# A transformer layer with a mixture of experts: gate, up and router products in plain fp32, expert weights held in SBUF

## The reference, cut to what matters

```
x  = x + ln(attention(ln(x)) @ Wout) * g_out
lg = (x @ wt.T + cond @ wg.T) / 2               # router, 8 logits a token
gp = leaky(einsum('th,ehm->etm', x, w_gate))    # 8 experts, h = 256, m = 128
up = einsum('th,ehm->etm', x, w_up)
y  = sum over the two best experts of weight * ((gp * up) @ w_down)
y += (leaky(x @ sw_gate) * (x @ sw_up)) @ sw_down    # shared, 256 wide = 2 blocks
x  = x + y
```

## Time and profile before

| | us |
|---|---|
| median of 3 runs | 1060.0 (1059.67 to 1060.96) |
| the profiled execution, its own time | 1064.17 |
| its span, first to last instruction | 1062.4 |
| mean granted TensorE clock | 0.994 of full |

### The profile page before, as it was taken

How to read it: one execution, slowest core, us unless ns; L and a number is a source line. 1 busy time by engine, 2 the same in 40 slices (tenths; PEclk the granted TensorE clock), 3 DMA queues, 4 the chain that set the end, 5 groups by cost and what they waited for, 6 DMA issues and landing times.

```text
span 1062.4 us, 21427 instructions
## 1 busy us (share of the span) xinstructions
PE 1014.6 (96%) x6788; PEld 815.3 (77%) x6788; DVE 707.4 (67%) x2457; ACT 526.5 (50%) x1564; POOL 437.0 (41%) x422
## 2 busy tenths in 40 slices
PE   3887999999999999999999999999999999999998
PEld 2665877778777887778777787777877788777877
DVE  8789577665867558665676647676576755856543
ACT  3488346651565435663456614665246643565220
POOL 1634154441554333642535515454245534444212
PEclk9899999999999999999999999999999999999999
DMA  5316414112132013311132212311123211232043
GB/s 198 80 54 215 151 60 122 53 66 63 61 110 90 28 55 101 100 61 61 43 118 72 71 42 79 112 65 46 62 66 113 82 41 41 84 106 71 20 138 102
DMA packets 40996, 87.68 MB, mean 83 GB/s; under 512 B 4192, under 2 KB 19040, under 8 KB 40624
## 3 DMA queue, kind: packets, MB, share of 16 engines
q1 hardware_dynamic: 39920, 83.57, 24.5%
q10 hardware_dynamic: 960, 2.62, 0.7%
HBM read 76.57 MB, written 9.60 MB: 81 GB/s over the span
## 4 chain that ended last, share of the span: by engine, by line
PE 75%; DVE 10%; issue 5%; ACT 4%; DVEq 0%; POOL 0%; ACTq 0%
PE psY L1641 13%; PE psS L1511 6%; PE psO L1547 5%; PE psG L69 5%; PE psG L71 5%; PE psG L70 5%; PE psT L1522 5%; PE psS L71 3%; PE psS L70 3%; PE psS L69 3%; PE psS L1507 3%; PE psT L1529 2%; PE psO L1550 2%; PE psT L69 2%; PE psT L71 2%
## 5 line engine op out<-in xcount | busy, mean ns | idle before, releaser
L604 POOL TENSOR_TENSOR work<-work,rden 128x514 f32<-128x514 f32 x128 | 134.0, 1047 | 322.3 <-DVE rden L1137 321.6
L1641 PE MATMUL psY<-Wd,H 128*128 128x256 f32 x640 | 172.5, 399 | 0.0
L763 ACT ACTIVATE work<-work,low 128x257 f32<-128x257 f32 x256 | 128.5, 504 | 60.1 <-DVE low L1155 59.5
L69 PE MATMUL psG<-x1T_hi,Wgu 128*128 128x512 f32 (+1 forms) x292 | 134.8, 462 | 2.6 <-ACT leaky L807 1.9
L1641 PEld LDWEIGHTS psY<-Wd,H 128*128 128x128 f32 x640 | 112.4, 190 | 29.4 <-issue 14.4
L1155 DVE CUSTOM_DVE_ANT_0 work<-psS,bias,null_s 128x256 f32<-128x256 f32 x256 | 113.3, 480 | 28.4 <-PE psS L1511 25.9
L1251 DVE SCALAR_TENSOR_TENSOR leaky<-leaky 128x512 f32<-128x512 f32 x80 | 56.4, 704 | 101.5 <-ACT leaky L807 100.5
L71 PE MATMUL psG<-x1T_lo,Wgu 128*128 128x512 f32 (+1 forms) x292 | 114.9, 394 | 0.0
L70 PE MATMUL psG<-x1T_hi,Wgu 128*128 128x512 f32 (+1 forms) x292 | 114.4, 392 | 0.0
L593 POOL TENSOR_TENSOR rq<-qss,neghalf 128x16 f32<-128x16 f32 x32 | 97.5, 3048 | 36.3 <-DVE qss L1131 36.3
L1511 PE MATMUL psS<-KB,qT 64*128 64x256 f32 (+1 forms) x1024 | 105.7, 325 | 0.0
(11 more groups left out here) (259 smaller groups left out, 2306.7 us busy)
## 6 DMA issues: line engine op xcount, KB each, us to landing
Wgu<-wexp SPq DMA_DIRECT2D x80, 512.0 KB, 3.4
Wb<-wscr SPq DMA_DIRECT2D x64, 256.0 KB, 3.6
wexp<-Wgu SPq DMA_DIRECT2D x10, 512.0 KB, 2.9
xres<-in_x SPq DMA_DIRECT2D x8, 512.0 KB, 4.7
xin<-in_x SPq DMA_DIRECT2D x7, 512.0 KB, 4.2
out<-work SPq DMA_DIRECT2D x7, 512.0 KB, 2.9
H<-in_wgu SPq DMA_DIRECT2D x10, 256.0 KB, 3.9
bias<-bscr SPq DMA_DIRECT2D x4, 512.0 KB, 6.6
```

The costliest lines, as they stand in the source:

```text
L69: te.matmul(dst, a_hi, b_hi, start=start, stop=False)
L604: pool.tensor_tensor(T1[sl][:, hs, :], T1[sl][:, hs, :], rden[sl][:, 1, hs].unsqueeze(2) .to_broadcast([P, 2, N + 1]), ALU.mult)
L763: act.activation(T1[sl][:, h, :], T1[sl][:, h, :], ACT.Exp, scale=-1.0, bias=low[sl][:, 1, h:h + 1], accum_out=den[sl][:, 1, h:h + 1])
L1641: mm = te.matmul(psY[:, t // 2, (t % 2) * D:(t % 2 + 1) * D], H[:, k % H_RING, t * P:(t + 1) * P], Wd[:, ORDER[k], :], start=(k == 0 and t ...
```

## The change: what it does

The parts, `wexp`, the ring, the splits in round 0 and the rounds' weight loads go. The ten blocks of raw fp32 weights are loaded once into `Wgu` (ten DMAs of 256 KB, right behind the load of round 1's x), and PE waits for all ten once, between round 0 and the loop. x1 turned is one fp32 tensor: ACT copies its first chunk out of PSUM, DVE its second. A gate or up product is four plain fp32 matmuls, two halves of 256 tokens by two chunks; a half in the last round is two. The router product is two plain fp32 matmuls of 512 columns with 8 stationary columns, and its turn uses the identity. The DVE preparations of the router's parts and of I2 go.

```diff
-        x1T = [sb(f"x1T_{part}", [P, KC, TOK], F32R) for part in PARTS]
-        Wgu = sb("Wgu", [P, W_RING, 2, 2, KC, P], F32R)
+        x1T = sb("x1T", [P, KC, TOK])
+        Wgu = sb("Wgu", [P, BLOCKS, 2, KC, P])
...
-            def load_weights(m, k):
-                former = k - W_RING if k >= W_RING else max(range(k, BLOCKS, W_RING)) - BLOCKS
-                need(sp, u_ps, m, former + 1)
-                stand(sp, waited_sp)
-                sp.dma_start(Wgu[:, k % W_RING].bitcast(F32), wexp.ap()[ORDER[k]]).then_inc(wgu_ld[k % W_RING].sem, 16)
...
-            for e in range(BLOCKS + 2):
-                if e < BLOCKS:
-                    if e >= H_RING:
-                        sp.wait_ge(parts_done.sem, e - H_RING + 1)
-                    sp.dma_start(H[:, e % H_RING, :], wgu[e].rearrange("p w c m -> p (w c m)")) \
-                        .then_inc(wraw_in[e % H_RING].sem, 16)
...
+            for k in range(BLOCKS):
+                sp.dma_start(Wgu[:, k], wgu[ORDER[k]]).then_inc(ld_gu.sem, 16)
...
-                        act.activation(Wgu[:, e % W_RING, 0], H[:, e % H_RING, :].rearrange(
-                            "p (w c m) -> p w c m", w=2, c=KC), ACT.Copy).then_inc(lead_done.sem, 1)
...
-                for c, bank in ((0, psG), (1, psO)):
-                    need(act, x1T_ps, m, c + 1)
-                    act.activation(x1T[0][:, c, :], bank[:], ACT.Copy).then_inc(x1T_a.sem, 1)
+                need(act, x1T_ps, m, 1)
+                act.activation(x1T[:, 0, :], psG[:], ACT.Copy).then_inc(x1T_a.sem, 1)
...
-                        dve.tensor_tensor(Wgu[:, e % W_RING, 1], H[:, e % H_RING, :].rearrange(
-                            "p (w c m) -> p w c m", w=2, c=KC), Wgu[:, e % W_RING, 0].bitcast(F32),
-                            ALU.subtract).then_inc(parts_done.sem, 1)
...
-            def x1_parts(m):
-                for c, bank in ((0, psG), (1, psO)):
-                    need(dve, x1T_a, m, c + 1)
-                    dve.tensor_tensor(x1T[1][:, c, :], bank[:], x1T[0][:, c, :].bitcast(F32),
-                                      ALU.subtract).then_inc(x1T_v.sem, 1)
+            def x1_turned(m):
+                need(dve, x1T_ps, m, 2)
+                dve.tensor_copy(x1T[:, 1, :], psO[:]).then_inc(x1T_v.sem, 1)
...
             def logits(m, last=False):
                 for c in range(KC):
-                    te.matmul(logit_bank(last), WtP[:, c, :], x1T[0][:, c, :], start=(c == 0), stop=False, skip_group_check=True)
-                for c in range(KC):
-                    mm = te.matmul(logit_bank(last)[0:E, :], WtP[:, c, 0:E], x1T[1][:, c, :], start=False, stop=(c == KC - 1),
-                                   skip_group_check=True)
+                    mm = te.matmul(logit_bank(last), Wt[:, c, :], x1T[:, c, :], start=(c == 0), stop=(c == KC - 1))
...
             def gate_up(m, k, w, bank):
-                for c in range(KC):
-                    mm = products(te, bank, [Wgu[:, k % W_RING, part, w, c, :] for part in range(2)],
-                                  [part[:, c, :] for part in x1T], c == 0, c == KC - 1)
+                for half in range(2):
+                    cols = half_tokens(half)
+                    for c in range(KC):
+                        mm = te.matmul(bank[:, cols], Wgu[:, k, w, c, :], x1T[:, c, cols], start=(c == 0), stop=(c == KC - 1))
                 return mm
...
             attention(0, None, 1)
+            te.wait_ge(ld_gu.sem, 16 * BLOCKS)
             with te.Fori(1, ROUNDS - 1) as r:
```

More of the change, by code:

```diff
@@ L287, in logit_bank @@
         def logit_bank(last):
-            return psY[0:2 * E, 1, :] if last else psO[0:2 * E, :]
+            return psY[0:E, 1, :] if last else psO[0:E, :]
         def weight_bank(last):
@@ L330, in attention_moe @@
         bias_in = [events(f"bias_in{i}", 0) for i in range(BIAS_PARTS)]
[L331 to L334, removed]
+        ld_gu = events("ld_gu", 0)
         xin_in = events("xin_in", 16)
@@ L906, in kv_parts @@
             def kv_parts():
[L907 to L910, removed]
+                hi, lo = (part[:, :, KV0:Q0] for part in Wall)
+                pre(dve.tensor_copy(hi, Wkvn_in))
+                pre(dve.tensor_tensor(lo, Wkvn_in, hi.bitcast(F32), ALU.subtract))
                 n = wall_trail(slice(0, KC), Q0, 2 * P)
@@ L1000, in attention @@
                 if moe is not None:
[L1001 removed]
+                    x1_turned(moe)
                 else:
[L1003 removed]
                     positions_norm(8, 4, V_SILU1)
@@ L1565, in turn_half @@
                 if half > 0:
-                    need(te, x1T_v, m, KC * half)
+                    need(te, x1T_a, m, half)
+                    need(te, x1T_v, m, half)
                 for c in range(KC):
@@ L1572, in block_half @@
             def block_half(m, k, w, half):
-                need(te, wgu_ld[k % W_RING], m, 16 * (k // W_RING + 1))
-                need(te, x1T_v, m, KC * (half + 1))
+                need(te, x1T_a, m, half + 1)
+                need(te, x1T_v, m, half + 1)
                 cols = half_tokens(half)
@@ L1597, in turn_logits @@
                 for t in range(TILES):
-                    mm = te.matmul(psY[:, 0, t * E:(t + 1) * E], LT[:, t * P:(t + 1) * P], I2, start=(t == 0), stop=True,
+                    mm = te.matmul(psY[:, 0, t * E:(t + 1) * E], LT[:, t * P:(t + 1) * P], ident[0:E, 0:E], start=(t == 0), stop=True,
                                    skip_group_check=True)
```

63 lines of the change are left out of this document (14 added, 49 removed).

## The result

The changed kernel takes 1108.99 us (median of 4 runs, 1108.63 to 1110.24) against 1060.01 us of the kernel before, run beside it: a ratio of 1.0452, 95% interval 1.0440 to 1.0465 (the two medians themselves give 1.0462). The forecast was 1106, with a range of 1096 to 1118. The profiled execution of the changed kernel took 1108.63 us, its span is 1106.8.

What follows compares the result with a forecast made beforehand. PE, 96% busy and 75% of the chain, was taken to bound the kernel. Loop +44.4, tail +6.6, round 0 -4.5, prologue -0.4 sum to +46.1; 1064.2 becomes 1110.3, less 4.2 excess gives 1106 us, range 1096 to 1118.

Steps and rivals of the forecast that it cites:

- The price of a product: Gate or up product on PE: 1.39 to 1.73 us in the loop, 0.34 more; 0.365 more in the tail.
- The router product: Router product on PE in each round: 0.93 to 1.73 us, +0.80, taken at the same price by column.
- Hidden in the q stage: Per round, 1.25 us of the q stage's six products' 2.04 falls into PE's waits; bounds 0 and 2.04.
- The tail: After the rounds: dearer products, partly covered by waits for x1 and the router, add 6.6 us; bounds +4 and +8.
- Round 0 and the prologue: Splits gone from ACT and DVE in round 0: -4.5 us, bounds -8 and 0; router's part instructions gone: -0.4.
- the forecast's own sign: Test for round 0: the forecast is wrong if round 0 doesn't end 4 to 6 us earlier.
- the floor of a step: Round 0's steps: PE's own work in a step is some 2.6 us, against steps of 2.8 to 3.4.
- The split in halves at nothing: Gate and up products in two halves of 256 columns: costed at nothing, since a record's price follows its columns.
- More hidden: Rival: DVE chain sets the q stage's length, all 2.04 us vanish, perhaps round 0's 6 won; 1097 us, chance 0.12.
- A price of the gate's place: Rival: new gate and up records also pay fp32r's 0.0155 us; 0.12 a product, +20, 1126 us; chance 0.08.
- Faster than before: Rival: a fp32 matmul costs one record's time, a product 0.865 us; about 70 us less, 985; chance 0.02.
- Weights late: Rival: weights arrive late at PE's one wait between round 0 and the loop; +0 to 5, chance 0.01.

Runs made afterwards that it cites:

- second profile of before: The kernel before, unchanged, profiled once more: 1059.61 us, span 1058.0.
- a round alone with it: The kernel before with only the router product made two plain fp32 matmuls in place of four fp32r: 1070.08 us, ratio 1.0093.
- first profile of before: The kernel before, unchanged, in the profiled execution that the prediction worked from: 1064.2 us, span 1062.4.
- whole products: The changed kernel with each gate and up product as two matmuls of 512 columns in place of four of 256: 1103.48 us, ratio 1.0412.
- products 42.9: The kernel before with only the gate and up products made plain fp32 in halves, on the hi parts: 1102.5 us, ratio 1.0408.
- 32 instructions that compute nothing: The kernel with whole products plus 32 idle PE instructions in each of the loop's rounds: 1108.39 us, ratio 1.0446.
- without the stream: The kernel before with the rounds' weight loads left out, the ring loaded once with three blocks: 1061.21 us, ratio 1.0009.
- ups whole: The changed kernel with gates still in halves and ups as whole products of 512 tokens: 1106.95 us, ratio 1.0450.

## Why the prediction was right, point by point

The direction, the mechanism and most of the size came out; one term, that of round 0 and the prologue, was too large. The fair comparison is the changed kernel against the second profile of before: spans of 1106.8 and 1058.0, +48.8 where the sum had +46.1.

- **The price of a product**, 1.39 to 1.73: right. The Trainium skill ("TensorE: Matmul & The Clock Gate", "Back-to-back issue gap") gives N/2.4 + 2.5 ns as the gap of a single matmul, 216 ns for 512 columns. A plain fp32 record takes 0.216 us here but moves 256 columns, for which the formula gives 109 ns, so the prediction's "the trace agrees for the fp32 records" is an agreement of the number and not of the rule. For fp32r with 512 columns the trace has 0.23, and the +0.43 a product that the prediction worked out from the page is not what was measured.
- **The router product**, +0.80: too low by 0.1 in its records, and by 0.2 as a round alone with it grew by 1.01.
- **Hidden in the q stage**, 1.25: right, 1.24 measured. In the steps some 0.3 more were hidden, which the forecast didn't have; this and the router nearly cancel. A round of the loop grew by 6.19 (forecast 6.35). The seventh, which the forecast took as one more of the same, grew by 7.11: with no next round's work beside it less was hidden, as its third score moved by 3.06 us and that of the others by 2.59. Together 6 x 6.19 + 7.11 = 44.2, forecast 44.4.
- **The tail**, +6.6: +6.8. The router's wait became 0.91 shorter, forecast 0.9.
- **Round 0 and the prologue**, -4.5 and -0.4: this is the term that was mis-sized. Against the first profile of before the loop starts 5.1 us earlier, close to the forecast's 4.9, but that is luck: 2.9 of it is what that profile lost to the second one in stretches of lowered clock. Against the second one it is 2.2, and the forecast's own sign (round 0 ends 4 to 6 us earlier) fails. The missing 2.7 have three parts. Round 0 became 3.4 shorter (81.77 to 78.39) and not 4.5. The steps from the eighth on gave back 2.7 and the stretch behind them 0.5, where the forecast had 4.3: the floor of a step, put at "some 2.6 us", is 2.77 to 2.79, which the steps ahead of the splits already showed in the first profile (2.77), and 0.2 had been given for a clock that was at 1.00 there in both later profiles. The router's parts gave no 0.4 back: in profiles without lowered clock PE's first score stands at 49.8 to 50.2 us with them and at 50.0 to 50.2 without. And the changed kernel's profile has lowered clock at the end of its prologue, which cost the other 1.2 (first score at 51.3). This term is the whole difference between 46.1 and 48.8.
- **The split in halves at nothing**: wrong, though hidden in the sum. "A record's price follows its columns" holds to 0.015 us a product (1.73 and 1.72). What the argument did not see is the number of instructions. It hardly shows in the total, because the kernel before pays the same wait at its heads (up to 1.17 us from start to start in its second profile): the change kept it where whole products would have removed it.
- **The rivals.** More hidden: no, rounds would be near 131 by the DVE chain, and PE is without gaps instead. A price of the gate's place: no, eight records in 1.73 beside down's 1.73. Faster than before: no, 1280 records of gate and up, and 1.73 a product. Weights late: no, the ten loads are issued from 46.6 to 52.5 us, land 8.9 later, and no wait of PE names them.
- **The range.** Its bounds were said to be taken at some two thirds; for the upper side that gives 1116 where 1114 stands. The measured 1109 lies inside either.

By the medians, each against the kernel before beside it, the parts add up roughly: products 42.9, router 10.5, together 53.4, less 49.0 measured leaves 4.4 for the splits and the preparations that went. The traces give round 0 3.4; single medians can carry a microsecond or so of lowered clock at the two ends.

## What to carry to other kernels

Where PE is busy for 98% of a loop, price an exchange of matmul forms by start-to-start distances of the same form elsewhere in the trace, and let only those idle gaps of PE cover it that can be walked through one by one. Where several engines are nearly full, what an edit gives back ends at the next limit: read that floor from steps beside it that the edit doesn't touch (2.77 us here, not 2.6). Profile twice before subtracting an execution's excess, to see where it lay. And look at the instruction queue of the engine that is the bound: an "issue" wait at a loop's head together with a queue that fetches in every round says that the loop's body is too long, and instructions that compute nothing count against that length too.

## What the runs showed of the hardware

- PE's loop body has a limit beyond which every jump back fetches it anew: 20 packets (0.33 MB) below it, 65 to 67 (1.06 to 1.10 MB) above, nine packets for each jump back, and 0.5 to 1.3 us from start to start at a head in place of 0.23. 32 instructions that compute nothing cost 0.76 us a round.
- A plain fp32 product with 8 or 16 stationary columns costs 1.81 to 1.82 us for two matmuls of 512, no less than with 128 (1.72 in the kernel with whole products).
- Stretches of lowered clock came and went from one execution to the next in the prologue, round 0 and the tail, and in no profile in the seven rounds behind round 0. Such a stretch moved the loop's start by about 0.5 to 1.6 us: the kernel with whole products shows 0.83 over 90 to 100 us and a round 0 of 79.99, the one with ups whole 1.00 and 78.40, though PE waits 1.13 and 1.14 us for DVE in that window of either.
- Halving HBM reads, from 76.6 to 36.2 MB, changed no round (125.59 with and without the stream).
